# The first batch's context: half loaded in the preparation, half at the start of cross-attention

## The reference

```python
x = x + xattn(layernorm(x), ctx)     # per batch b:
q = einsum('btd,dhk->bthk', layernorm(x), Wq) + bq      # 16 heads of 64
k = einsum('bsd,dhk->bshk', ctx, Wk) + bk
v = einsum('bsd,dhk->bshk', ctx, Wv) + bv
probs = softmax(einsum('bshk,bthk->bhts', k, q / 8))
out = einsum('bthk,hkd->btd', einsum('bhts,bshk->bthk', probs, v), Wo) + bo
```

## Time and profile before

| | us |
|---|---|
| median of 3 runs (lowest, highest) | 3262.93 (3259.77, 3263.29) |
| the profiled execution | 3259.59 |
| its span | 3257.8 |
| TensorE busy | 3059.9 (94%) |
| VectorE busy | 1683.3 (52%) |
| ScalarE busy | 1445.1 (44%) |
| GpSimd busy | 115.1 (4%) |

### The profile page before, as it was taken

The page is one execution under the profiler, slowest core; times in us unless marked ns, Lnnn a source line. Parts: engine busy times, 40 slices in busy tenths (PEclk is TensorE's granted clock), DMA queues, the critical chain, the costliest instruction groups (busy, mean ns, idle before and its releaser), DMA issues. The chain is left out here.

```text
span 3257.8 us, 61769 instructions
## 1 busy us (share of the span) xinstructions
PE 3059.9 (94%) x25814; PEld 2672.7 (82%) x25814; DVE 1683.3 (52%) x2786; ACT 1445.1 (44%) x2978; POOL 115.1 (4%) x87
## 2 busy tenths in 40 slices
PE   6899999999999999999999999999989789969997
PEld 5788888888888888888888888888746689959997
DVE  5355655565565556556565655656533765530001
ACT  3355555555555555555555555555532420011111
POOL 0000000000000000000000000000040320100000
PEclk9799999999999999999999999999999855579998
DMA  7311221121122112112211211211270000217661
GB/s 310 110 51 39 75 65 44 44 75 52 39 75 65 45 47 77 46 39 77 63 45 56 78 39 48 78 41 41 51 172 1 17 33 0 96 56 282 251 227 60
DMA packets 234822, 253.18 MB, mean 78 GB/s; under 512 B 22328, under 2 KB 169944, under 8 KB 234096
## 3 DMA queue, kind: packets, MB, share of 16 engines
q1 hardware_dynamic: 233040, 241.79, 23.2%
q0 software_dynamic: 1280, 4.20, 0.4%
q10 hardware_dynamic: 288, 4.19, 0.3%
HBM read 215.42 MB, written 34.70 MB: 77 GB/s over the span
## 5 line engine op out<-in xcount | busy, mean ns | idle before, releaser
L272 PE MATMUL fills<-wv_group,ctxT_hi 128*128 128x256 f32 x4096 | 777.1, 285 | 1.3 <-DVE ctxT_lo L477 0.6
L280 PE MATMUL fills<-ctxT_hi,wk_pairs 128*128 128x512 f32 x2048 | 703.9, 405 | 0.6 <-DVE keys L492 0.6
L272 PEld LDWEIGHTS fills<-wv_group,ctxT_hi 128*128 128x128 f32 x4096 | 644.6, 189 | 24.2 <-issue 20.3
L492 DVE SCALAR_TENSOR_TENSOR keys<-fills,bk,keys 64x512 fp32r<-64x512 f32 x512 | 383.8, 750 | 407.5 <-ACT keys L409 403.8
L272 PE MATMUL fills<-wv_group,ctxT_lo 128*128 128x256 f32 x2048 | 571.9, 279 | 0.0
L409 ACT ACTIVATE keys<-fills,bk 64x512 fp32r<-64x512 f32 x512 | 349.5, 683 | 404.4 <-PE fills L280 401.1
L280 PEld LDWEIGHTS fills<-ctxT_hi,wk_pairs 128*128 128x128 f32 x2048 | 385.6, 188 | 102.9 <-issue 23.9
L280 PE MATMUL fills<-ctxT_lo,wk_pairs 128*128 128x512 f32 x1024 | 401.3, 392 | 0.0
L485 DVE TENSOR_TENSOR values<-fills,values 128x512 fp32r<-128x512 f32 x256 | 176.6, 690 | 416.7 <-ACT values L404 416.7
L272 PEld LDWEIGHTS fills<-wv_group,ctxT_lo 128*128 128x128 f32 x2048 | 387.0, 189 | 0.0
L529 DVE TENSOR_TENSOR probsT<-probsT_ps,probsT 128x512 fp32r<-128x512 f32 x504 | 348.2, 691 | 67.4 <-ACT probsT L441 58.8
(11 more groups left out here) (210 smaller groups left out, 2999.4 us busy)
## 6 DMA issues: line engine op xcount, KB each, us to landing
e_w<-in_L_ffn_W SPq DMA_DIRECT2D x64, 1024.0 KB, 8.8
ctx_stage<-in_ctx SPq DMA_DIRECT2D x128, 256.0 KB, 2.9
wv_group<-wv_split SPq DMA_DIRECT2D x64, 512.0 KB, 4.7
wk_pairs<-wk_split SPq DMA_DIRECT2D x128, 256.0 KB, 3.3
q<-q_split SPq DMA_DIRECT2D x256, 64.0 KB, 2.7
q_split<-p_qb SPq DMA_DIRECT2D x16, 512.0 KB, 3.8
o_parts<-o_half SPq DMA_DIRECT2D x128, 64.0 KB, 1.9
a_ua<-o_parts SPq DMA_DIRECT2D x32, 256.0 KB, 5.4
```

The lines of the kernel that those rows point to most:

```text
L272: last = nc.tensor.matmul(pJ[:, bank[0], 256 * k:256 * k + 256], c[:, t, s:s + P], wv[:, w, t, :], start=t + n == 0, stop=t == DT - 1 and ...
L280: last = nc.tensor.matmul(pJ[:, bank[0], :], wk[:, p, w, t, :], c[:, t, 512 * j:512 * j + 512], start=t + n == 0, stop=t == DT - 1 and n == 2)
L492: last = nc.vector.scalar_tensor_tensor(out=keys[lo_rows(j), x, 512 * j:512 * j + 512], in0=pJ[DK * a:DK * a + DK, bk_, :], scalar=bk_sb[h ...
```

## The change

`prepare` and `cross_attention` share a new object `FirstContext`. It holds a tile `ctx_first` for all 16 row blocks of the first batch's context (32 KB per partition), in a new space `key_space` just below `shared`. The same space holds, earlier, x (`p_x`, the first half) and the query buffers (`p_qb`, the second half), and later the `keys`. `p_wp` moves into `shared`, where the transposed context comes later. In `prepare`, SP waits until all eight row blocks of x are normalised and issues the loads of context blocks 0 to 7, ahead of the query stores. It no longer waits for stores at the end of the block. In `cross_attention`, SP issues the bias, then waits for the query and weight stores, issues blocks 8 to 15 without further waits, and then the value weights. TensorE reads the first batch's blocks from `ctx_first`, after a semaphore for blocks 0 to 7 (all eight together), one for 8 to 11 and one for 12 to 15. ScalarE waits for the weight stores before its first eviction. The later batches use the ring as before. In the diff, headings between @@ say which part is meant; it is cut to what matters.

```diff
@@ cross_attention: names, places @@
-def cross_attention(nc, ctx, ..., row_scale, shared, early, xo, x_bv, aw, used,
+def cross_attention(nc, ctx, ..., row_scale, shared, key_space, first, early, xo, x_bv, aw, used,
...
-        keys = sb("keys", [P, XG, S], F32R)
+        keys = nc.alloc_sbuf_tensor_at("keys", [P, XG, S], F32R, offset=key_space)
...
         def ctx_load(sp, b, u):
+            if b == 0:
+                first.load(sp, ctx, u)
+                return
             sp.dma_start(stage[:, u % NS, :], ctx[b, P * u:P * u + P, :]).then_inc(ctx_in[u % NS], 16)
@@ cross_attention, SP's start @@
-            for u in range(NS):
+            for n in range(4):
+                sp.wait_ge(first.q_out[n], 16 * 4)
+            sp.wait_ge(first.w_out, 64)
+            for u in range(ST // 2, ST):
                 ctx_load(sp, 0, u)
-            for u in range(NS, ST):
-                sp.wait_ge(filled, u - NS + 1)
-                ctx_load(sp, 0, u)
-                if u == NS + 1:
-                    wv_load(sp, 0)
+            wv_load(sp, 0)
             wk_load(sp, 0, 0)
@@ cross_attention, TensorE @@
             def ctx_fill(no, b, u):
 
-                pe.wait_ge(ctx_in[u % NS], 16 * (ST // NS * b + u // NS + 1))
-                pe.wait_ge(fill_lo, no - 1)
+                if b:
+                    pe.wait_ge(ctx_in[u % NS], 16 * (ST // NS * (b - 1) + u // NS + 1))
+                else:
+                    first.wait(pe, u)
+                if no >= 2:
+                    pe.wait_ge(fill_lo, no - 1)
                 for t in range(DT):
-                    last = nc.tensor.transpose(pJ[:, bank[0], P * t:P * t + P],
-                                               stage[:, u % NS, P * t:P * t + P], ident[:, :])
+                    rows = stage[:, u % NS, P * t:P * t + P] if b else first.rows[:, u, P * t:P * t + P]
+                    last = nc.tensor.transpose(pJ[:, bank[0], P * t:P * t + P], rows, ident[:, :])
                 last.then_inc(filled, 1)
...
             for u in range(ST):
                 bank[0] = u % 2
-                if u >= 2:
-                    ctx_fill(u, 0, u)
-                else:
-                    pe.wait_ge(ctx_in[u], 16)
-                    for t in range(DT):
-                        last = nc.tensor.transpose(pJ[:, u, P * t:P * t + P], stage[:, u, P * t:P * t + P], ident[:, :])
-                    last.then_inc(filled, 1)
+                ctx_fill(u, 0, u)
@@ cross_attention, ScalarE @@
             act.wait_ge(bias_in, 32)
+            act.wait_ge(first.w_out, 64)
             for u in range(ST):
                 fill_hi_ctx(u, u % 2, u)
@@ new, and prepare @@
+class FirstContext:
+
+    def __init__(self, nc, key_space, sem):
+        self.rows = nc.alloc_sbuf_tensor_at("ctx_first", [P, ST, D], F32, offset=key_space)
+        self.landed = [sem("ctx_first0"), sem("ctx_first1"), sem("ctx_first2")]
+        self.w_out = sem("p_w_out")
+        self.q_out = [sem(f"p_q_out{n}") for n in range(4)]
+
+    def load(self, sp, ctx, u):
+        sp.dma_start(self.rows[:, u, :], ctx[0, P * u:P * u + P, :]).then_inc(self.landed[max(u // 4 - 1, 0)], 16)
+
+    def wait(self, pe, u):
+        pe.wait_ge(self.landed[max(u // 4 - 1, 0)], 64 if u >= ST // 2 else 128)
...
-        xs = sb("p_x", [P, B, D], F32)
+        xs = nc.alloc_sbuf_tensor_at("p_x", [P, B, D], F32, offset=key_space)
...
-        w_p = sb("p_wp", [P, 2, 2, DT, WX], F32R)
+        w_p = nc.alloc_sbuf_tensor_at("p_wp", [P, 2, 2, DT, WX], F32R, offset=shared)
...
-        qb = sb("p_qb", [P, 4, 4, 2, P], F32R)
+        qb = nc.alloc_sbuf_tensor_at("p_qb", [P, 4, 4, 2, P], F32R, offset=key_space + 4 * B * D)
@@ prepare, SP @@
             sp.dma_start(raw[:, 0, :, :], wv.rearrange("(t p) h k -> p t (h k)", p=P)).then_inc(w_in[1], 16)
+            sp.wait_ge(normed, B)
+            for u in range(ST // 2):
+                first.load(sp, ctx, u)
             for n in range(16):
                 half, pair = n // 8, n % 8
                 sp.wait_ge(q_parts, n + 1)
                 sp.dma_start(q_split[P * pair:P * pair + P, 4 * half:4 * half + 4, :, :],
                              qb[:, n % 4, :, :, :].bitcast(F32)).then_inc(q_out[n % 4], 16)
-            sp.wait_ge(w_out, 64)
-            for n in range(4):
-                sp.wait_ge(q_out[n], 16 * 4)
@@ perceiver @@
+        keys_space.enter_context(nc.sbuf_tensor("key_space", [P, XG * S], F32, side="right"))
         shared = SBUF_END - 4 * 2 * DT * S
+        key_space = shared - 4 * XG * S
+        first = FirstContext(nc, key_space, lambda n: new_semaphore(nc, n, used))
...
+        keys_space.close()
```

More of the change, by code:

```diff
@@ L56, in add, with cross_attention @@
                                 ALU.add).then_inc(self.added, 1)
-def cross_attention(nc, ctx, wk_split, wv_split, q_split, bk, ident, o_parts, row_scale, shared, early, xo, x_bv, aw, used,
+def cross_attention(nc, ctx, wk_split, wv_split, q_split, bk, ident, o_parts, row_scale, shared, key_space, first, early, xo, x_bv, aw, used,
                     batches=B):
@@ L303, in score @@
                                                PRO + fill_no(16 * g - 16 + 11 + 4 * (i // 2), last) + 1))
-                if h or not first[0]:
+                if h or not fresh[0]:
                     pe.wait_ge(exped, 64 * b + 4 * h)
@@ L338, in weigh @@
                 last.then_inc(weighed, 1)
-            first = [True]
+            fresh = [True]
             def batch(b, last):
@@ L385, in _ @@
                     score(0, 0)
-                    first[0] = False
+                    fresh[0] = False
                 bank[0] = m % 2
@@ L575, in norm_steps, with prepare @@
     step(nc.vector.bn_aggr(mv[:, t, :], stats[:, t, :]))
-def prepare(nc, x, wq, bq, wk, wv, ident, wk_split, wv_split, q_split, used):
+class FirstContext:
[8 more added lines that the diff above has]
+        pe.wait_ge(self.landed[max(u // 4 - 1, 0)], 64 if u >= ST // 2 else 128)
+def prepare(nc, x, ctx, wq, bq, wk, wv, ident, wk_split, wv_split, q_split, shared, key_space, first, used):
     es = ExitStack()
@@ L606, in prepare @@
         w_in = [sem("p_w_in0"), sem("p_w_in1")]
-        w_out = sem("p_w_out")
-        q_out = [sem(f"p_q_out{n}") for n in range(4)]
+        w_out, q_out = first.w_out, first.q_out
         made = sem("p_made")
@@ L1825, in perceiver @@
     with nc.sbuf_tensor("ident", [P, P], F32) as ident:
-        prepare(nc, x, xWq, xbq, xWk, xWv, ident, wk_split, wv_split, q_split, used)
-        shared_space, small = ExitStack(), ExitStack()
+        shared_space, keys_space, small = ExitStack(), ExitStack(), ExitStack()
         shared_space.enter_context(nc.sbuf_tensor("shared", [P, 2 * DT * S], F32, side="right"))
+        keys_space.enter_context(nc.sbuf_tensor("key_space", [P, XG * S], F32, side="right"))
         shared = SBUF_END - 4 * 2 * DT * S
+        key_space = shared - 4 * XG * S
+        first = FirstContext(nc, key_space, lambda n: new_semaphore(nc, n, used))
+        prepare(nc, x, ctx_1024, xWq, xbq, xWk, xWv, ident, wk_split, wv_split, q_split, shared, key_space, first, used)
         early = Early(nc, shared, lambda n, shape: small.enter_context(nc.sbuf_tensor(n, shape, F32)),
                       lambda n: new_semaphore(nc, n, used))
-        cross_attention(nc, ctx_1024, wk_split, wv_split, q_split, xbk, ident, o_parts, row_scale, shared, early, xWo, xbv,
+        cross_attention(nc, ctx_1024, wk_split, wv_split, q_split, xbk, ident, o_parts, row_scale, shared, key_space, first, early, xWo, xbv,
                         (aWq, aWk, aWv), used)
+        keys_space.close()
         with ExitStack() as kept:
```

## The result

The changed kernel takes 3253.86 us (median of 10 runs, 3249.57 to 3259.01) against 3261.48 (10 runs, 3258.88 to 3263.29): ratio 0.9976, 95% interval [0.9967, 0.9984]. Timed again with the first experiments (11 runs, median 3254.53 against 3260.49): 0.9982 [0.9973, 0.9991]. So 6.0 to 7.6 us are gained; forecast were 7.1. Both intervals leave out 1: even their ends nearest to it are 5.2 and 2.9 us of gain.

A forecast was written before the change was run, and what follows sets the result against it. Bound taken: a chain of latencies at the seam between preparation and cross-attention. Earlier eviction 4.35 + stall 2.8 = 7.15 us, other terms 0; 3262.93 - 7.1 = 3255.8 us, range 3250 to 3260.5.

The forecast's parts named there:

- The end of the preparation: SP's 2.2 us wait for the last store leaves the block, so the bias is issued at 79.4 instead of 81.69.
- The bias is late next: In cross-attention the bias lands at 82.95; ScalarE's first eviction moves from 87.45 to 83.1, gaining 4.35 us (0.5 to 4.5).
- Rival C: At cross-attention's start the bias lands no earlier than near 86; only 3.8 us gained, 3259.1; chance 0.11.
- The stall: TensorE's wait for context blocks behind the 1 MB of value weights goes: 2.8 us gained.
- The cover in the preparation: Eight context loads in the preparation fill a hole in DMA traffic before the query stores; cost 0, at most 2 us.
- The clock: TensorE at half clock until six microseconds into the dense work, as before; taken as 0, 2 us either way.
- B: TensorE's full clock holds through the seam, gaining 13.1 us, 3249.8; chance 0.08.
- E: First loads disturb the preparation, at worst 3 us late at its end; 4 us gained, 3258.9; chance 0.05.
- D: Keys' new SBUF place slows score matmuls or key writes in all batches; 2% costs 8.5 us; chance 0.04.
- The size: Total gain at the seam between preparation and cross-attention: 7.15 us, 7.1 in round.

The follow-up runs named there:

- the first experiments: First group of follow-up runs, in which the unaltered changed kernel was timed once more: median 3254.53 against 3260.49 us for the kernel before.
- waits_back: Changed kernel with the waits for the stores put back at the end of the preparation; median 2.3 us above the changed kernel measured beside it.
- bias_fixed: Changed kernel with the key bias loaded in the preparation into its own place, other tiles unmoved; median 1.5 to 2.1 us below the changed kernel's two.
- wv_first: Changed kernel with the value weights issued before the late context blocks; run once, first value fill at 102.64 us.
- wv_later: Kernel before with the value weights issued after context block 11 instead of 5; first value fill 108.42 us, the medians show nothing.
- four_fixed: Changed kernel with the bias loaded in the preparation and the first batch's context blocks on four PSUM banks instead of two; 15.7 us below before.
- keys_right: Kernel before with only the keys moved to the changed kernel's place on SBUF's right side; median 2.8 us above before, ratio 1.0005.
- changed: The kernel with the whole change described, against the kernel before: 3253.86 against 3261.48 us, ratio 0.9976.
- bias_early: Changed kernel with the key bias loaded in the preparation, which also moved tiles on the left up 64 bytes; 18 us slower than before.
- four-bank kernels: The four_fixed kernel and its copies with 32 or 128 bytes of unused SBUF ahead of the left tiles; the copies 21.6 and 17.4 us slower.

## Why the prediction was right

- **The end of the preparation**: from the end of the last store's issue (78.71) to the bias's 0.4 us were shown, 0.5 taken; 79.11 for 79.4. Confirmed by `waits_back`, which gives 2.1 us back.
- **The bias is late next**: landing 3.0 us for 2.8, eviction 82.93 for 83.1, so 4.52 us gained there for 4.35. `bias_fixed` shows it as cause: without it 79.64. Rival C, which let it land near 86, is out.
- **The stall**: 2.76 us gone for 2.8, with no wait at block 8. The reason given, the weights ahead of the block that is wanted, was half of it: the order can stay if the lead is there (`wv_first`), and changing it returns only 0.5 us without (`wv_later`).
- **The cover in the preparation**: held. SP's issues were cheaper than 0.65 us each (3.65 for eight), and VectorE's wait of 4.9 did not move; E is out.
- **The clock**: half from 81 to 108.4, 5.8 us into the value fills, as before; B did not come in the changed kernel. But one of my reasons against it was read wrongly. The stage at 2660 us, which I called one of transposes, is matmuls of three columns (the line below, of the kernel before), and `four_fixed` shows transposes alone bringing the clock back when nothing lies between them. So what kept it down was the idle time between the pairs, and B was nearer than its 0.08 for any version that packs it. In the changed kernel the clock fell near 81.0, inside the 4.24 us that TensorE waits for the first evictions. Short gaps then kept it down: 0.64 us of idle ahead of every pair, at half clock for 19 us. The Trainium skill, page "TensorE: Matmul & The Clock Gate", section "Why this matters for your kernels", has full clock lost to idle gaps between bursts of matmuls; the fall near 81.0 agrees. The same section of the Trainium skill has the advice to keep TensorE busy without a break if it is to get its full clock; `four_fixed` agrees.

```profile
2661.27 0.88 PE L1253 MATMUL c_pV<-c_cp,c_atp 128*128 128x3 bf16 x27
```

- **D**: the keys' place did no harm that a run shows (score matmuls 420 for 417 ns, and above; `keys_right` leaves room for up to 4.6 us). But I had put its price at nothing by an argument, two sides of SBUF with like durations, which says nothing of small shifts: 64 bytes on the left cost 27 us, more than three times what the change gains. That the tiles of the changed kernel lie well is luck as far as this forecast goes.
- **The size**: 7.28 us at the first value fill (4.52 and 2.76) for 7.15. The totals, 7.6 and 6.0, lie on either side of it; cross-attention (3 us) and the last stretch (3.7 us) vary by more between traces, so that they come so near is in part chance. The median, 3253.86, is 1.9 us below the 3255.8 forecast, of which 1.45 is that the kernel before came out at 3261.48 in ten runs instead of 3262.93 in three.

## What to carry to other kernels

At a seam between two blocks, write down which event the first instruction of each engine waits for, and move the next-latest into the DMA traffic's holes ahead of it; here these were the stores, the context, the stall behind the weights, and then the bias. Here a prefetched lead made the order of the later loads harmless, while reordering alone moved the stall. When a tile is added or moved, compare busy time and mean of the unchanged matmuls before judging the edit: here a mean moved by 2 to 5 ns, or 10 us more busy time at the same mean, was the places, and a fixed offset for the new tile brought the old pace back.

## What the runs showed of the hardware

- Moving the tiles on one side of SBUF by 32, 64 or 128 bytes made cross-attention 24, 27 and 19 us longer (2369.8, 2370.7 and 2364.8 against 2340.7 to 2347.0 without) with the same instructions; how the loss is shared among the fills differs by shift.
- By stretches of 300 us, the value fills' median moves between 276 and 281 ns within one execution and between executions of one kernel (`changed`: 281 up to 970 us, 276 to 278 after); after the shift of 64 bytes it is 283 throughout (`bias_early`). Why it moves is open.
- With transposes back to back TensorE's clock rose to 2.4 GHz after some 3 us (79.87 to 82.8, `four_fixed`); at 2.58 us a pair it stayed at 1.2 GHz for 19 us although 13.77 of 19.40 us were busy.
- An idle gap of 2.7 us ahead of the same transposes left the clock at full in two of three executions of the four-bank kernels (1.06 us for 8) and at half in the third (1.94).
